# Layer four's attention: the order of stages within one step of the loop over units

## What is computed

```python
def attention(q, k, v, mask):
    scores = jnp.einsum('bhqd,bhkd->bhqk', q, k) / jnp.sqrt(jnp.float32(HD))
    scores = scores * mask - 10000.0 * (1.0 - mask)
    probs = jax.nn.softmax(scores, axis=-1)
    return jnp.einsum('bhqk,bhkd->bhqd', probs, v)
```

## Time and profile before

| | us |
|---|---|
| runs, not profiled | 2045.20, 2050.21, 2052.34 |
| their median | 2050.21 |
| the profiled execution | 2044.37 |
| its span, first to last instruction | 2042.6 |
| mean granted TensorE clock | 0.979 |
| busy in the span: TensorE, VectorE, ScalarE, GpSimd | 1849.2, 1151.9, 973.4, 771.2 |

### The profile page before, as it was taken

How to read it: one execution, slowest core, us unless ns; L and a number is a source line. 1 busy time by engine, 2 the same in 40 slices (tenths; PEclk the granted TensorE clock), 3 DMA queues, 4 the chain that set the end, 5 groups by cost and what they waited for, 6 DMA issues and landing times.

```text
span 2042.6 us, 38530 instructions
## 1 busy us (share of the span) xinstructions
PE 1849.2 (91%) x15569; PEld 1566.9 (77%) x15569; DVE 1151.9 (56%) x2106; ACT 973.4 (48%) x2551; POOL 771.2 (38%) x819
## 2 busy tenths in 40 slices
PE   6788887898999999999999999999998788888798
PEld 4566665787888888888888888888877666666587
DVE  3444555445555555566665555556544677776743
ACT  4344444333444444444444444444444576675733
POOL 3322232402433435254353433425231476675500
PEclk9999999999999999999999999999999899998999
DMA  3000001101322223132231322222120000000000
GB/s 113 11 7 2 7 2 43 50 1 16 70 45 58 58 47 65 34 67 43 42 63 37 68 46 54 57 48 53 38 90 1 12 2 2 7 2 6 2 21 21
DMA packets 163201, 71.98 MB, mean 35 GB/s; under 512 B 136512, under 2 KB 154576, under 8 KB 163024
## 3 DMA queue, kind: packets, MB, share of 16 engines
q1 hardware_dynamic: 150672, 50.64, 12.6%
q10 hardware_dynamic: 12352, 18.88, 3.0%
HBM read 33.84 MB, written 2.10 MB: 18 GB/s over the span
## 4 chain that ended last, share of the span: by engine, by line
PE 75%; DVE 10%; ACT 9%; issue 3%; POOL 2%; DMA 1%; SPq 0%; ACTq 0%; DVEq 0%; POOLq 0%
PE ps_high L197 40%; PE ps_four L197 8%; PE ps_four L2667 5%; PE ps_four L2655 5%; PE ps_high L2552 2%; PE ps_high L2591 2%; ACT l_pt L1738 2%; PE ps_high L2446 1%; ACT l_sm L1783 1%; DVE l_sm L2173 1%; DVE l_sm L2183 1%; PE ps_four L2462 1%; ACT l_prob L1829 1%; PE ps_four L2467 1%; PE ps_high L2602 1%
## 5 line engine op out<-in xcount | busy, mean ns | idle before, releaser
L1839 ACT ACTIVATE l_ao<-ps_four,columns 128x512 fp32r<-128x512 f32 x128 | 88.0, 687 | 388.2 <-PE ps_four L2667 377.6
L1626 POOL TENSOR_TENSOR l_prob<-l_prob,l_mx 128x516 f32<-128x516 f32 x128 | 134.2, 1049 | 310.1 <-DVE l_mx L2214 310.1
L1829 ACT ACTIVATE l_prob<-ps_four,l_mx 128x129 f32<-128x129 f32 x512 | 181.8, 368 | 123.0 <-DVE l_mx L2207 122.8
L197 PE MATMUL ps_high<-l_hT,l_wq 128*128 128x512 f32 x768 | 210.8, 410 | 2.1 <-DVE l_hT L2096 2.1
L197 PEld LDWEIGHTS ps_high<-l_wo,l_ao 128*128 128x128 f32 x1536 | 198.0, 190 | 10.6 <-issue 0.7
L197 PE MATMUL ps_high<-l_wo,l_ao 128*128 128x256 f32 x1536 | 202.7, 281 | 0.0
L197 PE MATMUL ps_high<-l_wv,ctxT 128*128 128x512 f32 x768 | 200.3, 396 | 1.4 <-ACT l_qT L1810 1.4
L197 PE MATMUL ps_high<-ctxT,l_wk 128*128 128x512 f32 x768 | 198.5, 394 | 0.0
L1592 POOL TENSOR_TENSOR l_sm<-l_sm,l_mask 128x1024 f32<-128x1024 f32 x64 | 158.8, 2504 | 38.0 <-DVE l_sm L2173 38.0
L2220 DVE COPY l_planes<-l_prob 128x1024 uint16<-128x1024 uint16 x128 | 88.8, 694 | 149.0 <-POOL l_prob L1626 149.0
L197 PEld LDWEIGHTS ps_high<-ctxT,l_wk 128*128 128x128 f32 x768 | 144.8, 189 | 33.7 <-DVE l_V L2195 0.4
(11 more groups left out here) (295 smaller groups left out, 3791.5 us busy)
## 6 DMA issues: line engine op xcount, KB each, us to landing
l_staging<-in_L_xattn_wv ACTq DMA_DIRECT2D x8, 512.0 KB, 4.2
l_staging<-in_L_xattn_wk ACTq DMA_DIRECT2D x8, 512.0 KB, 4.2
l_staging<-in_L_xattn_wq ACTq DMA_DIRECT2D x8, 512.0 KB, 4.1
l_staging<-in_L_xattn_wo ACTq DMA_DIRECT2D x8, 512.0 KB, 3.9
ctx_tok<-in_ctx SPq DMA_DIRECT2D x8, 256.0 KB, 3.2
x_tok<-in_x SPq DMA_DIRECT2D x4, 512.0 KB, 5.8
l_raw_w<-in_L_xattn_mlp_w SPq DMA_DIRECT2D x2, 1024.0 KB, 6.9
l_planesT<-l_planes SPq DMA_TRANSPOSE x128, 3.1
```

The source lines that it names most:

```text
L197: ins = e.matmul(out, a, b, start=start and i == 0, stop=stop and i == 2, skip_group_check=not check)
L1626: e.tensor_tensor(pr[:, :, 0:S + 1], pr[:, :, 0:S + 1], mx[:, 3, :].unsqueeze(2).to_broadcast([P, GB, S + 1]), ALU.mult).then_inc(sem("poo ...
L1829: ins = e.activation(pr.t[:, b, 0:S + 1], banks[b // 2].t[:, (b % 2) * (S + 2):(b % 2) * (S + 2) + S + 1], ACT.Exp, bias=mx[:, 1, b:b + 1] ...
L1839: e.activation(ao.t[:, 0, :], bk.t, ACT.Identity, bias=self.cols(f"L2_xattn_bv{at + 1}")[:, hd:hd + 1]).then_inc(sem("act.l2_values"), 1)
```

## The change

Within one step of the loop, `shifted(n-1)` is emitted ahead of deal A instead of behind it, and `scores(n+1)` behind the second deal instead of ahead of the transposes of unit n-2. No instruction is added or taken away.

```diff
@@ -1280,14 +1280,14 @@
         for n in range(N + 2):
             if n < N:
                 masked(n)
-            fill()
             if 1 <= n <= N:
                 shifted(n - 1)
-            if n + 1 < N:
-                scores(n + 1)
+            fill()
             if n >= 2:
                 probs(n - 2, 1)
             fill()
+            if n + 1 < N:
+                scores(n + 1)
             if 1 <= n <= N:
                 probs(n - 1, 0)
                 shifted_too(n - 1)
```

## The result

The changed kernel is slower. Its median is 2054.68 us (20 runs, 2048.44 to 2062.93), that of the kernel before 2046.68 (20 runs, 2043.25 to 2052.34); the ratio is 1.0037, with a 95% interval of 1.0026 to 1.0048, some 7.6 us. I had forecast 2045.9 and a small gain. The time lies inside my range, but the direction was wrong.

The account below looks back on a forecast made before the run. No engine was full; hand-overs between TensorE, VectorE and ScalarE in layer four's attention were taken to bound it. Gains 14.7 less costs 10.4 gave 4.3 us off the median 2050.2: 2045.9 us, range 2036 to 2058.

Parts of the forecast that it names:

- Shift ahead of deal A: VectorE's shift no longer waits behind dealt work: gains 1.8 (step 10), 1.3 (24), 2.0 (25), 2.6 (28); step 14 left out.
- Ports: Rival: SBUF exclusion with GpSimd's mask additions draws the five moved shifts out to 3.40 us each; 2056.8 us, chance 0.06.
- Transposes under the scores' wait: Second heads' transposes run while TensorE waits for VectorE's multiplication ahead of scores: gain 3.0 us, bounds 0 and 5.8.
- The 1.0 for step 30: Transposes of unit 28 go under the 3.69 us that TensorE waits for the norm: gain 1.0 us.
- What it costs, first: Scores now come behind TensorE's waits for ScalarE in steps 2, 8, 12, 16, 20, 23: 6 x 1.10 = 6.6 us.
- Deals of steps 2 and 27: Keys of group a2 go 2 stages late, the last norm 3 stages later; both priced at nothing.
- The cover that I named: Dealt stages end two steps before attention does, hiding displaced deals; without it each costs 1 to 4 us.
- What it costs, second: Scores lengthen TensorE's loop in light steps from 5.07 to 6.17 us, over VectorE's 5.79; ten steps cost 3.8 us.
- Clock: Shorter waits leave TensorE less at 1.2 GHz in steps 25 and 28: gain 3.0 us, bounds 0 and 5.
- The lengthened loop binds: Rival: scores between second and first transposes set the pace; 2060.6 us, or 2053 with half the gains; chance 0.18.
- both of its signs: Wait for ScalarE's shift ahead of transposes grows from 5.4 to over some 15 us; multiplications wait for scores behind dealt matmuls.

Follow-up runs that it names:

- e1: Kernel before with only the shift moved ahead of deal A, scores left in their old place: 2035.2 us, ratio 0.9947.
- h1: Kernel before with the shift early in steps 25 and 28 only: 2043.62 us, ratio 0.9976.
- f2: e1 with scores behind deal B only in the nine steps where B holds TensorE work (2, 8, 12, 16, 20, 21, 23, 24, 27): 2057.21 us.
- g2: e1 with scores behind deal B only in the projection steps 2, 12, 21, 24 and 27: 2044.78 us, ratio 0.9988.
- i2: e1 with scores behind deal B only in steps 2 and 27, whose deals are displaced: 2043.5 us, ratio 0.9985.
- f4: e1 with scores directly behind the second heads' transposes only in steps 7, 10, 15, 19, 22 and 25: 2040.47 us, ratio 0.9957.
- e3: e1 with scores behind the second heads' transposes but still ahead of deal B, in every step: 2041.95 us, ratio 0.9975.
- g1: e1 with scores behind deal B only in the norm steps 8, 16, 20 and 23: 2044.33 us, ratio 0.9983.
- f1: e1 with scores behind deal B only in the 22 steps where B holds nothing for TensorE: 2037.48 us, ratio 0.9944.
- f3: e1 with the scores also moved ahead of deal A, directly behind the shift: 2050.11 us, ratio 1.0006.

## Why the prediction was wrong

**Shift ahead of deal A: right by itself.** I priced 7.7 us for it and 3.0 for the clock, most of that in steps 25 and 28. Alone it gave 10.9 (e1). Beside late scores, where my sum has it, it is worth 3.9. The split was less good: steps 25 and 28 were priced 4.6 and up to 3.0 of clock and gave 4.9 (h1); steps 10, 14 and 24 were priced 3.1 and left about 6 by the times. The traces do not put it there: up to masked(25) e1 has gained 2.2 us on before, and 2.6 more come in step 27, of which h1 has 0.8.

**Ports: this rival did not come, with one exception.** The line L2183, which answers to the earlier trace rows, after and then in e1:

```profile
L2183 DVE TENSOR_TENSOR l_sm<-l_sm,l_mx x32: 1224/1234/3394, 1615.8 to 1934.0; 128x1024 f32<-128x1024 f32 x32
```

```profile
L2183 DVE TENSOR_TENSOR l_sm<-l_sm,l_mx x32: 1224/1256/3400, 1607.9 to 1910.6; 128x1024 f32<-128x1024 f32 x32
```

The median fell from 1482 ns to 1234, or 1256, and the longest stayed at 3.4 us. The five moved shifts (steps 10, 14, 24, 25, 28) took 1.57, 2.88, 2.65, 1.23 and 2.70 us before, and 1.23 to 1.30 after (1.22 to 1.89 in e1); the rival had 3.40 for each. The exception is a shift that did not move, that of step 29: 3.23 us in after, f2, g2 and i2, which have the shift early and the scores of step 27 late, and 1.22 to 1.77 in all others. In these four, masked(30) follows masked(29) after 7.8 us, in e1 after 6.0. The Trainium skill's page "SBUF — State Buffer", section "SBUF: two separate sides", states an exclusion by which a shift would wait for a GpSimd addition. The trace of after agrees: an addition of the mask runs from 1909.03 to 1911.38, this shift starts 0.20 us behind its start and ends 1.08 behind its end, and the next addition, which starts before the shift is done, takes 3.35 us in place of 2.4. No run takes the additions away.

**Transposes under the scores' wait: nothing that shows.** Priced at 3.0. TensorE's wait for L2173 fell by 12.8, so they did go under it, but neither f4 nor e3 shows a gain from it; f4's interval of some 4 us leaves room for a small one. The 1.0 for step 30 did not come either: the norm's second half slipped behind the transposes, by the very displacement in step 27 that I had priced at nothing.

**What it costs, first: this is the step that failed.** I priced the scores behind deal B at one set of scores, 1.10 us, for each of six steps, 6.6, and wrote of what follows them that VectorE's next multiplication would be served "early enough". That was argued for light steps only. Where B holds matmuls, the multiplication waits for the whole of B: ScalarE's rows, the projection, the half clock behind the wait. The nine steps cost 19.9 us (f2) where six were priced 6.6: the norm steps 7.4 (g1) against 4.4, the projections 8.4 (g2) against 2.2. Some 6 us of it come already from the scores standing behind the second transposes, for which TensorE waits on ScalarE, and some 13 from passing deal B (e3 between f1 and the change). I had counted what TensorE has to do longer, and not what VectorE has to wait. Put together, the late scores cost 18.4 us where I had 10.4 less the 4.0 of what they were to gain, and that turned the sign: 10.9 gained and 18.4 lost are the 7.5 that the change is slower.

**Deals of steps 2 and 27: priced at nothing; the one of step 27 costs.** i2's 7.8 us (4.4 in the trace) hold the scores' own share in both steps, and no run has the displacement alone. Step 2's 2.4 are the order of scores and transposes, since e3 has them without displaced keys. In step 27 some 3.0 are left, and 1.8 in the drawn-out shift of step 29. The cover that I named, that the chain of dealt stages ends early, does not help where a dealt copy stands on VectorE ahead of masked(28). My price for lost cover, a projection alone, 1 to 4 us each, would have been near.

**What it costs, second: there, with no cost that shows.** The light steps did lengthen, as worked out to 6.17. Transposes of three light steps in after lie 6.23 and 6.28 us apart, where the earlier trace rows have 5.79:

```profile
1635.72 1.04 PE L2591 MATMUL ps_high<-ident,l_sm 128*128 128x128 f32 x8
...
1641.95 1.09 PE L2591 MATMUL ps_high<-ident,l_sm 128*128 128x128 f32 x8 [1.19 <-ACT l_sm L1783]
...
1648.23 1.09 PE L2591 MATMUL ps_high<-ident,l_sm 128*128 128x128 f32 x8 [1.19 <-ACT l_sm L1783]
```

I took 3.8 us; f1, which has the same loop, lost none against e1 that can be told. But f1 also holds what the transposes under the wait were to gain, 3.0, so what it measures is the two together: 0.8 by my prices, -0.6 with some 5 to either side. That the loop by itself is free, because the next full step takes it up, is my reading.

**Clock: no gain.** 0.92 before and after. In step 25 the scores took 1.83 behind a wait of 2.17, where the earlier trace rows have 2.02 behind 3.04; steps 12 and 23 paid 2.50 and 0.92 behind new waits. Without the late scores it did come: 0.93 in e1, with 3.0 us less busy time (269.8 to 266.8).

**The rivals.** "The lengthened loop binds" had direction and near enough the size (2060.6, or 2053 with half of the gains), and both of its signs came true: 19.8 for ScalarE's shift, over 15, and multiplications that wait for scores behind dealt matmuls. But the two signs were two mechanisms. The loop after which I named it shows no cost (f1); the loss sits in the steps of the second, which I had mentioned as a mark of the first (f2). I gave it 0.18.

**What stays open.** Why the early shift is worth only 3.9 us with late scores was not taken apart; the waits for banks that dealt additions and copies hold behind it (3.8 and 2.8 after, 1.7 and 1.6 in e1) are too small to be all, and so is the drawn-out shift of step 29 (1.8). The split of the 19.9 among single steps is rough.

**The best version.** e1, the early shift alone, beats both: 2035.2 us, 0.9947 of before. f1 and f4 are not told apart from it.

## What to carry to other kernels

A wait that runs beside other engines' needed work is no reserve: ask what the waiting instruction lets go first, not how long it waits. Before an instruction is moved behind a slot that is filled from elsewhere, go through every filling of that slot, and price each by what the consumer of the moved instruction waits, not by the moved instruction's own length; here that is 1.1 us against up to 8. Moving a short operation ahead of dealt work on its own engine paid here for the shift, whose inputs its own engine has just made, and not for the scores, which wait for another engine and hold the dealt work back behind that wait (f3, 12.1 over e1).

## What the runs showed that I had not expected

- Two executions can run in lockstep for long: with h1, whose first changed step is 25, the starts of masked(n) repeat those of before within 0.1 us over 247 us of attention, while the 1600 us ahead of it spread by 5.
- In step 12 of the change TensorE sat idle for 2.16 and 0.52 us, with eight transposes between, and then ran the keys' projection mostly at 1.2 GHz: 6.20 us in place of 3.70.
